# Converting a projection weight to bfloat16 one stage ahead, loading it on another queue, and issuing one input load ahead of a stage barrier

## The chip, the cores and the metric

The kernel runs on the 8 cores of one Trainium2 chip, as one program with no exchange between cores. Each core takes 1,024 query rows of one of two sequences; cores 0 to 3 hold sequence 0 and cores 4 to 7 sequence 1. The metric is the device time of the slowest core in microseconds (us), as the median of several runs.

## The reference, cut to what matters

```python
xn = _layernorm(x)                       # x: (2, 4096, 4096) float32
c_q = xn @ w_q_down                      # 4096 -> 1536
q_nope = c_q @ w_q_up_nope               # 32 heads x 128
q_rope = rope(c_q @ w_q_up_rope)         # 32 heads x 64
c_kv = xn @ w_kv_down                    # 4096 -> 512
k_rope = rope(xn @ w_k_rope)             # 4096 -> 64
q_lat = einsum('bhsd,hdr->bhsr', q_nope, wuk)
scores = q_lat . c_kv + q_rope . k_rope  # causal, / sqrt(192), softmax
out = (probs . c_kv) . wuv @ w_out
# FFN: router top-16 of 64, h = xn . A, out2 = (h * gates) . B
y = x + out + ffn(xn)
```

`w_kv_down` and `w_k_rope` lie side by side in one input called `wkvc`, 128 partitions x 32 x 576 values in float32 (9.44 MB; 4.72 MB as bfloat16). The tile for it in SBUF is `wkvcb`, in bfloat16.

## The kernel before, in words

Everything is emitted from Python into five in-order instruction lists (PE, DVE, ACT, POOL, SP) with semaphores. Transfers are issued by SP (`dma("sync", ...)`, queue q1, no conversion of type) and by POOL (`dma("gpsimd", ...)`, queue q0, which can convert float32 to bfloat16 on the way). Every transfer is spread over the core's 16 DMA engines. A helper on line 308 issues them all, so the profile has that one line for each; the tiles tell them apart.

The stages, in order of time in the profiled execution:

- 0 to 720 us: layer norm of the core's own rows, the projections to c_q, the router, the experts' first half, and `b_proj` for the 32 heads of q_nope (stage "qn"). For each head POOL loads a weight slice `wbuf<-wqn`; PE multiplies into one of two pairs of PSUM banks; `qn_evac` copies the pair to `qn_stg` on DVE (even heads) or ACT (odd heads), and SP stores that to DRAM (`qnope_scr<-qn_stg`). Each such copy waits on the semaphore `ysb` for *all* stores issued before it. `wqr_hook(oi)` is called after each slice load; at heads 3, 7, ..., 31 it makes POOL load one of eight parts of `wqrb`.
- 712 to 882 us: the rope half of q, for 8 blocks `tc` of 128 rows. SP loads two small tables (`ctab`, `stab`), PE multiplies into banks 0 to 3 (the banks that the last two q_nope heads used), DVE applies the rotation (lines 620 to 629), PE transposes (line 644), DVE and ACT in turn copy to `tr_stg`, and SP stores 128 KB (`qrope_scr<-tr_stg`). Here too each copy waits for all earlier stores (`ysb`).
- `stage_barrier()`: every engine waits until every semaphore has reached its count, those of all transfers too.
- 882 to 1547 us: stage A, over the 4,096 rows of the whole sequence, in 16 tiles of 256 rows. POOL loads `wkvcb` right behind the barrier. `emit_ln_stats_a` loads 128 rows of `xkv` (2 MB, as two halves) to `xbuf[slot]` on SP and takes the sums (DVE line 336, ACT lines 339 to 345); `emit_ln_stats_b` finishes the statistics and normalises (DVE line 385); `emit_ln_trans` transposes on PE (line 402) to `slabA`; `a_kv_tile` multiplies by `wkvcb` (lines 717, 721). Both chunks of a tile have their sums taken (`emit_ln_stats_a` twice) before the statistics of the first are finished.
- 1547 to 4660 us: a barrier, then attention over 32 heads; in its first 16 heads POOL converts `wout` and `b2` in DRAM to bfloat16 (`cast`, one after another on the semaphore `gc`).
- 4660 to 5286 us: a barrier, then the output projection and the experts' second half.

Of the kernel before, what the change touches and what calls it, by code (L numbers as in the profile page):

```python
# [10 lines left out]
BF16 = mybir.dt.bfloat16  # L11
# [83 lines left out]
def view3(t_ap, inner):  # L95
    n = t_ap.shape[1] // inner
    return t_ap.rearrange("p (c j) -> p c j", c=n)


def build_nc():  # L100
    nc = bass.Bass("TRN2", target_bir_lowering=False)

    def din(name, shape, dtype=F32):
        return nc.dram_tensor(name, list(shape), dtype, kind="ExternalInput").ap()

    XKV = din("xkv", (S_, D_))
# [4 lines left out]
    WKVC = din("wkvc", (128, 32, 576))  # L111
# [18 lines left out]
    KTS = nc.dram_tensor("ckvtm_scr", [128, S_ // 128, KVL_], BF16, kind="Internal").ap()  # L130
    ATS = nc.dram_tensor("attn_scr", [128, H_, NTOK], BF16, kind="Internal").ap()
    WOUTC = nc.dram_tensor("wout_c", [16, 128, 8192], BF16, kind="Internal").ap()
    B2C = nc.dram_tensor("b2_c", [16, 128, 2048], BF16, kind="Internal").ap()
    OUT = nc.dram_tensor("out_own", [NTOK, D_], F32, kind="ExternalOutput").ap()

    es = ExitStack()
    with es:
# [6 lines left out]
        kb = KB(sems)  # L144
# [31 lines left out]
        def pview(pool, name, shape, dtype, off):  # L176
            nbytes = int(np.prod(shape[1:])) * mybir.dt.size(dtype)
            assert off % 32 == 0, name
            assert off + nbytes <= pool.shape[1], (name, off, nbytes)
            base = nc.lookup_mloc(pool).addr  # L180
            return nc.alloc_sbuf_tensor_at(name, list(shape), dtype,
                                           offset=base + off)
# [12 lines left out]
        wkvcb = pview(pool1, "wkvcb", (128, 18432), BF16, 32768)  # L195
# [35 lines left out]
        xbuf = [pview(poolf, "xbuf0", (128, 4096), F32, 0),  # L231
                pview(poolf, "xbuf1", (128, 4096), F32, 16384)]
# [54 lines left out]
        def bank(i):  # L287
            return ps[i // 2][:, (i % 2) * 512:(i % 2) * 512 + 512]
# [7 lines left out]
        def t_run(fns):  # L296
            for f in fns[:-1]:
                kb.raw("tensor", f)
            return kb.t(fns[-1])
# [3 lines left out]
        def use(nm):  # L303
            uses[nm] = uses.get(nm, 0) + 1
            return uses[nm]

        def dma(eng, sem_name, out_ap, in_ap):
            kb.op(eng, lambda e, o=out_ap, i=in_ap: e.dma_start(out=o, in_=i),
                  inc=(sem_name, 16))
            return 16 * use(sem_name)  # L310
# [10 lines left out]
        lnfree = {("V", 0): 0, ("V", 1): 0, ("S", 0): 0, ("S", 1): 0}  # L321

        def R(nm, slot):
            return ST[nm + ("Z" if slot else "")]

        def emit_ln_stats_a(xsrc_row_ap, slot):
            sx = f"yx{slot}"
            kb.wait("sync", "V", lnfree[("V", slot)])
            kb.wait("sync", "S", lnfree[("S", slot)])
            dma("sync", sx, xbuf[slot][:, 0:2048], xsrc_row_ap[:, 0:2048])  # L330
            nl = dma("sync", sx, xbuf[slot][:, 2048:4096], xsrc_row_ap[:, 2048:4096])
            xb = xbuf[slot][:]
            kb.wait("vector", sx, nl)
            kb.drain("vector")
            kb.raw("vector", lambda e, xb=xb, slot=slot:
                   e.reduce_sum(R("xsum", slot), xb[:, 0:2048], AX))
            kb.wait("scalar", sx, nl)
            kb.drain("scalar")
            kb.raw("scalar", lambda e, xb=xb, slot=slot: e.activation(
                sqd[:], xb[:, 0:2048], ACT.Square, accum_out=R("xsqa", slot)))  # L340
            kb.drain("scalar")
            kb.raw("scalar", lambda e, xb=xb, slot=slot: e.activation(
                sqd[:], xb[:, 2048:4096], ACT.Square, accum_out=R("xsqb", slot)))
            kb.drain("scalar")
            s_sq = kb.s(lambda e, xb=xb, slot=slot: e.activation(
                sqd[:, 0:2048], xb[:, 2048:4096], ACT.Identity,
                accum_out=R("xsum2", slot)))
            lnfree[("S", slot)] = s_sq
            lnpend[slot] = (xb, s_sq)
# [67 lines left out]
        def stage_barrier():  # L417
            snap = dict(kb.cnt)
            for eng in KB.ENGS:
                for nm, v in snap.items():  # L420
                    kb.wait(eng, nm, v)

        xnfmB3 = view3(xnfmB[:], 1024)
        cq3 = view3(cqfm[:], 1024)
        for ch in range(8):
            emit_ln_stats_a(XOWN[ch * 128:(ch + 1) * 128, :], ch % 2)
            if ch > 0:
                vp = emit_ln_stats_b((ch - 1) % 2)
                emit_ln_trans((ch - 1) % 2, vp, xnfmB3, (ch - 1) * 128,
                              (4, 5, 6, 7))  # L430
# [49 lines left out]
        slot = 0  # L480
# [79 lines left out]
        b_proj(0, 8, xnfmB3, 32, None, cq_lhs, h_src, h_evac, "h")  # L560
        h_tm = kb.cnt["T"]

        def wqr_hook(oi):
            if oi % 4 == 3 and oi // 4 < 8:
                j = oi // 4
                if j == 0:
                    kb.wait("gpsimd", "T", h_tm)
                dma("gpsimd", "gq",
                    wqrb[:, j * 3072:(j + 1) * 3072],
                    WQR[j // 4][:, (j % 4) * 3072:(j % 4 + 1) * 3072])  # L570

        def qn_src(oi, slot):
            return (wbuf[slot][:, 0:1536], WQN[oi])
# [19 lines left out]
        for tc in range(8):  # L593
# [41 lines left out]
            for gi in range(4):  # L635
# [19 lines left out]
                dst = QRS[:, gi * 4:(gi + 1) * 4, tc * 128:(tc + 1) * 128]  # L655
                dma("sync", "ysb", dst, view3(tr_stg[sslot][:], 128))

        b_ysb = 16 * uses.get("ysb", 0)
        stage_barrier()

        slab3P = [view3(slabA2[0][:], 256), view3(slabA2[1][:], 256)]
        ckvfm3 = view3(ckvfm[:], 4096)
        wkv_loaded = dma("gpsimd", "g0", wkvcb[:], WKVC[:].rearrange("p c j -> p (c j)"))

        _gclast = [0]

        def cast(dst, srcw):
            if _gclast[0]:
                kb.wait("gpsimd", "gc", _gclast[0])
            _gclast[0] = dma("gpsimd", "gc", dst, srcw)  # L670

        lnfree[("V", 0)] = kb.cnt["V"]
        lnfree[("V", 1)] = kb.cnt["V"]
# [7 lines left out]
        def a_ln_stats_tile(t):  # L681
            for i4 in range(2):
                ch = t * 2 + i4
                emit_ln_stats_a(XKV[ch * 128:(ch + 1) * 128, :], ch % 2)
            return [emit_ln_stats_b((t * 2) % 2), emit_ln_stats_b((t * 2 + 1) % 2)]

        def a_ln_trans_tile(t, vxs):
# [7 lines left out]
        def a_kv_tile(t):  # L695
            slot = t % 2
            slab3 = slab3P[slot]
            tsl = t % 2
            kf = ktab_free[tsl]
            if kf:  # L700
                kb.wait("sync", kf[0], kf[1])
            dma("sync", f"yt{tsl}", view3(ktabc[tsl][:, 0:128], 64),
                COSK[t * 256:(t + 1) * 256, :].rearrange("(i p) j -> p i j", p=128))
            ktab_ns[t] = dma("sync", f"yt{tsl}", view3(ktabs[tsl][:, 0:128], 64),
                             SINK[t * 256:(t + 1) * 256, :].rearrange("(i p) j -> p i j", p=128))
            kb.wait("tensor", "g0", wkv_loaded)
            lv, ls = ln_done[t]
            kb.wait("tensor", "V", lv)
            kb.wait("tensor", "S", ls)
            kb.guard(0, 1, 2, 3, 4)  # L710
            fns = []
            for dc in range(32):
                for rc in range(4):
                    fns.append(lambda e, o=bank(rc)[:, 0:256],
                               l=view3(wkvcb[:], 576)[:, dc, rc * 128:(rc + 1) * 128],
                               r=slab3[:, dc, :], st=(dc == 0), sp=(dc == 31):
                               e.matmul(o, l, r, start=st, stop=sp))  # L717
                fns.append(lambda e, o=bank(4)[0:64, 0:256],
                           l=view3(wkvcb[:], 576)[:, dc, 512:576],
                           r=slab3[:, dc, :], st=(dc == 0), sp=(dc == 31):  # L720
                           e.matmul(o, l, r, start=st, stop=sp))  # L721
            tm = t_run(fns)
            kv_done[t] = tm
            return tm
# [103 lines left out]
        krdup_done = dma("sync", "ya", krdup[64:128, :], krdup[0:64, :])  # L828
        a_ysa = 16 * uses.get("ysa", 0)
        stage_barrier()  # L830

        ckvtm3 = view3(ckvtm[:], 512)
# [52 lines left out]
        def issue_loads(h):  # L885
# [8 lines left out]
            if h < 16:  # L894
                cast(WOUTC[h], WOUT[h])
                cast(B2C[h], B2[h])

# [373 lines left out]
        for dt in range(16):  # L1271
            ws = dt % 2
            gw = f"gw{ws}"
            kb.wait("gpsimd", "T", gw_free[ws])
            dma("gpsimd", gw, woutb[ws][:], WOUTC[dt])
            ngw = dma("gpsimd", gw, b2b[ws][:], B2C[dt])
            kb.wait("tensor", gw, ngw)
# [174 lines left out]
```

How the kernel before makes its waits and increments, by code:

```python
        def wrapped(e, fn=fn, h=h, amt=amt):  # L49
            fn(e).then_inc(h, amt)
# [3 lines left out]
    def wait(self, eng, nm, val):  # L54
        if val is None or val <= 0:
            return
        h = self.sems[nm]
        self.ops[eng].append(lambda e, h=h, v=val: e.wait_ge(h, v))
```

## Time and profile before

| what | us |
|---|---|
| median of 3 runs (5287.18 to 5734.02) | 5287.41 |
| the profiled execution | 5287.49 |
| its span on the slowest core (core 6) | 5286.0 |
| spans of the 8 cores | 5250.4 to 5286.0 |
| busy on the slowest core: PE / DVE / ACT | 4649.3 / 2305.2 / 1693.7 |

The span runs from the first to the last instruction of a core; the execution's own time is 1.5 us more. Busy shares are means over stages with different limits, so an edit is priced in its own stage, from what ends the waits there.

### The profile page before, as it was taken

What the parts mean: (1) busy time and instruction counts of PE and PEld (TensorE: products, weight loads), DVE (VectorE), ACT (ScalarE), POOL (GpSimd) and SP (SyncE); (2) the same over time, 40 slices, a digit from 0 to 9 for tenths busy, and PEclk for the clock granted to TensorE, in tenths of its full rate; (3) what the DMA queues carried; (4) which work ended last, traced back from release to release, by engine and by line L of the source; (5) the groups of instructions that cost most, each with busy time, mean ns of one, the idle gap of its engine ahead of it and who ended that gap; (6) DMA issues with size and microseconds to landing.
All of it is one profiled execution on the core that took longest, in us unless ns stands there. A gap on an engine that the chain in (4) does not pass through costs nothing.

```text
span 5286.0 us, 78953 instructions; the slowest of 8 cores (5250.4 to 5286.0 us)
## 1 busy us (share of the span) xinstructions
PE 4649.3 (88%) x27024; PEld 2202.6 (42%) x27024; DVE 2305.2 (44%) x4604; ACT 1693.7 (32%) x3075; POOL 100.5 (2%) x194
## 2 busy tenths in 40 slices
PE   1879874788858999999999999999999999969999
PEld 1434331444433444444444444444444444434444
DVE  3110032444424555555555555556555555511111
ACT  4100000454513444444444444444444444400000
POOL 0000000000000000000000000000000000000000
PEclk7889987899988999999999999999999999989999
DMA  4334734333336303303311000000000000054343
GB/s 129 64 54 89 128 69 88 105 137 112 133 116 89 49 5 53 53 6 48 53 24 30 13 13 1 13 13 1 13 13 13 1 13 5 1 166 129 124 136 104
DMA packets 151798, 318.09 MB, mean 60 GB/s; under 512 B 36736, under 2 KB 110720, under 8 KB 133440
## 3 DMA queue, kind: packets, MB, share of 16 engines
q0 software_dynamic: 24672, 137.38, 14.5%
q1 hardware_dynamic: 126752, 175.66, 10.2%
q8 instruction: 243, 3.98, 0.3%
q14 instruction: 131, 1.07, 0.1%
HBM read 363.59 MB, written 85.98 MB: 85 GB/s over the span
## 4 chain that ended last, share of the span: by engine, by line
PE 76%; DMA 9%; DVE 6%; issue 3%; ACT 3%; DVEq 2%; ACTq 0%; SPq 0%; POOL 0%; POOLq 0%
PE ps L1030 18%; PE ps L955 18%; PE ps L1294 8%; PE ps L717 6%; PE ps L458 6%; PE ps L961 5%; PE ps L1008 4%; DMA qnope_scr<-qn_stg 3%; PE ps L721 2%; PE ps L1302 2%; DVEq L61 2%; PE ps L964 2%; DMA xbuf<-xown 1%; DVE stats L973 1%; ACT probsb L994 1%
## 5 line engine op out<-in xcount | busy, mean ns | idle before, releaser
L955 PE MATMUL ps<-ckvfm,qlat 128*128 128x512 bf16 x4608 | 1111.0, 382 | 54.3 <-ACT probsb L994 29.7
L1030 PE MATMUL ps<-ckvtm,probsT 128*128 128x512 bf16 x4608 | 1102.1, 380 | 15.6 <-DVE stats L973 7.6
L994 ACT ACTIVATE probsb<-ps,stats 128x1024 bf16<-128x1024 f32 (+1 forms) x640 | 652.3, 1019 | 520.7 <-DVE stats L973 520.7
L1030 PEld LDWEIGHTS ps<-ckvtm,probsT 128*128 128x128 bf16 x4608 | 418.5, 98 | 599.1 <-issue 174.8
L955 PEld LDWEIGHTS ps<-ckvfm,qlat 128*128 128x128 bf16 x4608 | 421.3, 98 | 494.3 <-issue 104.7
L1294 PE MATMUL ps<-attn_cat,woutb 128*128 128x512 bf16 x2048 | 452.5, 382 | 40.1 <-DMA b2b<-b_c 26.8
L978 DVE TENSOR_REDUCE stats<-ps 128x1 f32<-128x1024 f32 (+1 forms) x384 | 419.1, 1092 | 35.6 <-issue 0.9
L1008 PEld LDWEIGHTS ps<-idb,probsb 128*128 128x128 bf16 x4608 | 309.7, 98 | 154.0 <-issue 6.8
L86 ACT COPY probsT<-ps 128x1024 bf16<-128x1024 bf16 x320 | 296.3, 926 | 227.6 <-PE ps L1008 227.5
L1008 PE MATMUL ps<-idb,probsb 128*128 128x128 bf16 x4608 | 361.9, 219 | 0.0
L961 PE MATMUL ps<-krdup,qropefm 64*128 64x512 bf16 x1152 | 358.7, 383 | 0.0
L717 PE MATMUL ps<-slabA,wkvcb 128*128 128x256 bf16 x2048 | 336.6, 290 | 9.2 <-DVE krf L758 7.5
L973 DVE TENSOR_REDUCE stats<-ps 128x1 f32<-128x1024 f32 (+1 forms) x256 | 296.5, 1158 | 102.1 <-PE ps L961 80.3
L1294 PEld LDWEIGHTS ps<-attn_cat,woutb 128*128 128x128 bf16 x2048 | 201.0, 98 | 279.1 <-issue 47.9
L402 PE MATMUL ps<-idb,xn_tm 128*128 128x128 bf16 x1280 | 105.6, 240 | 236.4 <-DVE xn_tm L385 201.0
L1317 DVE COPY dsb<-ps 128x512 f32<-128x512 f32 x64 | 41.3, 686 | 551.0 <-PE ps L1302 551.0
L458 PE MATMUL ps<-xnfmB,wbuf 128*128 128x512 bf16 x1280 | 278.6, 381 | 1.4 <-ACT xnfmB L86 1.4
L991 ACT ACTIVATE stats<-stats 128x1 f32<-128x1 f32 x384 | 77.9, 203 | 623.0 <-DVE stats L984 623.0
L1040 DVE SCALAR_TENSOR_TENSOR accb<-accb,stats,ps 128x512 f32<-128x512 f32 x192 | 143.5, 748 | 288.5 <-PE ps L1030 285.5
L85 DVE COPY probsT<-ps 128x1024 bf16<-128x1024 bf16 x320 | 201.6, 630 | 37.7 <-PE ps L1008 37.7
L458 PE MATMUL ps<-cqfm,wbuf 128*128 128x512 bf16 x768 | 177.5, 391 | 32.3 <-DMA wbuf<-wqn 26.0
L717 PEld LDWEIGHTS ps<-slabA,wkvcb 128*128 128x128 bf16 x2048 | 165.8, 101 | 94.5 <-issue 23.3
(144 smaller groups left out, 3856.1 us busy)
## 6 DMA issues: line engine op xcount, KB each, us to landing
xbuf<-xkv SPq DMA_DIRECT2D x64, 1024.0 KB, 10.3
wout_c<-wout POOLq DMA_DIRECT2D x16, 2048.0 KB, 21.1
woutb<-wout_c POOLq DMA_DIRECT2D x16, 2048.0 KB, 9.1
xbuf<-xown SPq DMA_DIRECT2D x16, 1024.0 KB, 7.0
xdb<-xown SPq DMA_DIRECT2D x64, 256.0 KB, 5.6
out_own<-outb SPq DMA_DIRECT2D x64, 256.0 KB, 2.4
wbuf<-wqd POOLq DMA_DIRECT2D x12, 1024.0 KB, 8.5
wbuf<-wqn POOLq DMA_DIRECT2D x32, 384.0 KB, 5.9
```

Of the source, the lines that this page charges most:

```text
L85: return e.tensor_copy(d, s)
L86: return e.copy(d, s)
L458: e.matmul(o, l, r, start=st, stop=sp))
L717: e.matmul(o, l, r, start=st, stop=sp))
L955: st=(rc == 0): e.matmul(o, l, r, start=st, stop=False))
L961: sp=(not diag): e.matmul(o, l, r, start=False, stop=sp))
L973: v_mx = kb.v(lambda e, b=nm4[i4x]: e.reduce_max(b, pp[:, 0:wid], AX, negate=True))
L978: kb.raw("vector", lambda e: e.reduce_max(ST["negmg"], pp[:, 0:wid], AX, negate=True))
L994: e.activation(o, i, ACT.Exp, bias=b, accum_out=l))
L1008: e.transpose(o, i, idb[:]))
L1030: e.matmul(o, l, r, start=st, stop=sp))
L1294: st=(fc == 0): e.matmul(o, l, r, start=st, stop=False))
```

## The change

Three edits. A DRAM tensor `WKVCC` takes a bfloat16 copy of `wkvc`, made by POOL with `cast` directly behind the last part of `wqrb`, in head 31 of the q_nope stage. Behind the barrier, SP (no longer POOL) loads `wkvcb` from `WKVCC` in two halves, before the loads of the second chunk of `xkv`. The first chunk of `xkv` is loaded by SP ahead of the barrier, behind the last store of the rope stage; for that, the barriers leave out the semaphores `yx0` and `yx1`.

```diff
+    WKVCC = nc.dram_tensor("wkvc_c", [128, 18432], BF16, kind="Internal").ap()
...
-        def emit_ln_stats_a(xsrc_row_ap, slot):
+        def emit_ln_stats_a(xsrc_row_ap, slot, preloaded=None):
             sx = f"yx{slot}"
-            kb.wait("sync", "V", lnfree[("V", slot)])
-            kb.wait("sync", "S", lnfree[("S", slot)])
-            dma("sync", sx, xbuf[slot][:, 0:2048], xsrc_row_ap[:, 0:2048])
-            nl = dma("sync", sx, xbuf[slot][:, 2048:4096], xsrc_row_ap[:, 2048:4096])
+            if preloaded is None:
+                ...
+            else:
+                nl = preloaded
...
             for eng in KB.ENGS:
                 for nm, v in snap.items():
+                    if nm in ("yx0", "yx1"):
+                        continue
                     kb.wait(eng, nm, v)
...
         def wqr_hook(oi):
...
                     wqrb[:, j * 3072:(j + 1) * 3072],
                     WQR[j // 4][:, (j % 4) * 3072:(j % 4 + 1) * 3072])
+                if j == 7:
+                    cast(WKVCC[:], WKVC[:].rearrange("p c j -> p (c j)"))
...
         b_ysb = 16 * uses.get("ysb", 0)
+
+        kb.wait("sync", "V", lnfree[("V", 0)])
+        kb.wait("sync", "S", lnfree[("S", 0)])
+        dma("sync", "yx0", xbuf[0][:, 0:2048], XKV[0:128, 0:2048])
+        a_pre_nl = dma("sync", "yx0", xbuf[0][:, 2048:4096], XKV[0:128, 2048:4096])
+
         stage_barrier()
...
-        wkv_loaded = dma("gpsimd", "g0", wkvcb[:], WKVC[:].rearrange("p c j -> p (c j)"))
+        kb.wait("sync", "gc", 16)
+        dma("sync", "ya", wkvcb[:, 0:9216], WKVCC[:, 0:9216])
+        wkv_loaded = dma("sync", "ya", wkvcb[:, 9216:18432], WKVCC[:, 9216:18432])
...
-                emit_ln_stats_a(XKV[ch * 128:(ch + 1) * 128, :], ch % 2)
+                emit_ln_stats_a(XKV[ch * 128:(ch + 1) * 128, :], ch % 2,
+                                preloaded=(a_pre_nl if ch == 0 else None))
...
-            kb.wait("tensor", "g0", wkv_loaded)
+            kb.wait("tensor", "ya", wkv_loaded)
```

The function `cast`, as before, waits on POOL for the previous cast and issues one converting transfer; it is only defined earlier in the file.

## Rows read from the trace of the kernel before

**Rows 1.** The page: busy share in 40 slices of 132 us, PE's clock.

```profile
PE   1879874788858999999999999999999999969999
...
PEclk7889987899988999999999999999999999989999
```

**Rows 2.** Busy time by stretch: engines (instructions), PE clock, DMA share, GB/s; stage A's start.

```profile
882.00:905.00 23.00, 0.00 (x0) 0.00 (x0) 0.00 (x0) 0.00 (x0) 0.72 (x1) 0.50 0.95 193
905.00:927.00 22.00, 0.00 (x0) 0.00 (x0) 2.38 (x2) 6.12 (x7) 0.00 (x0) 0.50 0.89 204
927.00:950.00 23.00, 7.69 (x65) 6.51 (x66) 13.81 (x22) 11.42 (x15) 0.00 (x0) 0.50 0.52 169
```

**Rows 3.** The chain that ended last, around the barrier: start us, us, what.

```profile
879.05 2.47 DMA qrope_scr<-tr_stg
...
881.94 0.34 SPq L308
...
883.27 43.49 DMA xbuf<-xkv
...
926.89 1.91 ACT sqd L339
...
949.93 1.01 PE ps L717 x4
```

**Rows 4.** A transfer issued in 882 to 884 us: engine, count, KB, us to landing.

```profile
wkvcb<-wkvc POOLq DMA_DIRECT2D x1, 4608.0 KB, 42.2
```

**Rows 5.** DMA queues in 966 to 979 us: GB/s in 40 slices; packets, MB, share.

```profile
GB/s 0 151 101 151 328 277 429 454 454 378 378 403 403 454 328 252 378 252 202 277 277 277 429 202 176 202 252 227 378 227 277 403 403 403 403 454 429 429 429 393
...
q1 hardware_dynamic: 572, 4.11, 95.4%
```

**Rows 6.** The same view, 1568 to 1582 us.

```profile
q1 hardware_dynamic: 129, 4.03, 97.2%
```

**Rows 7.** The chain that ended last, end of q_nope and start of rope.

```profile
712.59 2.13 DMA qnope_scr<-qn_stg
714.80 1.02 ACT qn_stg L86
...
716.73 2.19 DMA stab<-sinq
719.07 0.69 DVE tba L620
```

**Rows 8.** Timeline, same stretch: start, us, engine, line, operation [idle before <-what ended it].

```profile
701.89 0.54 POOL L308 DMA_DIRECT2D wqrb<-wqr  x1
...
714.80 1.01 ACT L86 CAST qn_stg<-ps 128x1024 bf16<-128x1024 f32 x1 [10.90 <-DMA qnope_scr<-qn_stg]
```

**Rows 9.** Transfers issued in 701 to 703 us, as in Rows 4.

```profile
wqrb<-wqr POOLq DMA_DIRECT2D x1, 768.0 KB, 9.0
```

**Rows 10.** A store issued in 703 to 704 us, beside that load.

```profile
qnope_scr<-qn_stg SPq DMA_DIRECT2D x1, 256.0 KB, 7.2
```

**Rows 11.** Two converting copies within DRAM, issued at 1662 and 1991 us.

```profile
wout_c<-wout POOLq DMA_DIRECT2D x1, 2048.0 KB, 19.9
...
wout_c<-wout POOLq DMA_DIRECT2D x1, 2048.0 KB, 23.1
```

**Rows 12.** DMA queues while such a copy runs, 1808 to 1822.5 us: packets, MB, share.

```profile
q0 software_dynamic: 48, 1.57, 83.7%
q1 hardware_dynamic: 48, 0.10, 2.0%
```

**Rows 13.** Transfers issued in 1802.5 to 1803.5 us, with such a copy among them.

```profile
wout_c<-wout POOLq DMA_DIRECT2D x1, 2048.0 KB, 22.5
attn_scr<-attnstg SPq DMA_DIRECT2D x1, 256.0 KB, 22.3
```

**Rows 14.** DMA queues while wkvcb loads, 890 to 920 us.

```profile
q0 software_dynamic: 224, 4.13, 81.9%
q1 hardware_dynamic: 222, 1.69, 18.0%
```

More of the change, by code:

```diff
@@ L324, in R @@
             return ST[nm + ("Z" if slot else "")]
-        def emit_ln_stats_a(xsrc_row_ap, slot):
+        def emit_ln_stats_a(xsrc_row_ap, slot, preloaded=None):
             sx = f"yx{slot}"
-            kb.wait("sync", "V", lnfree[("V", slot)])
-            kb.wait("sync", "S", lnfree[("S", slot)])
-            dma("sync", sx, xbuf[slot][:, 0:2048], xsrc_row_ap[:, 0:2048])
-            nl = dma("sync", sx, xbuf[slot][:, 2048:4096], xsrc_row_ap[:, 2048:4096])
+            if preloaded is None:
+                kb.wait("sync", "V", lnfree[("V", slot)])
+                kb.wait("sync", "S", lnfree[("S", slot)])
+                dma("sync", sx, xbuf[slot][:, 0:2048], xsrc_row_ap[:, 0:2048])
+                nl = dma("sync", sx, xbuf[slot][:, 2048:4096],
+                         xsrc_row_ap[:, 2048:4096])
+            else:
+                nl = preloaded
             xb = xbuf[slot][:]
@@ L561, in build_nc, with cast @@
         h_tm = kb.cnt["T"]
+        _gclast = [0]
+        def cast(dst, srcw):
+            if _gclast[0]:
+                kb.wait("gpsimd", "gc", _gclast[0])
+            _gclast[0] = dma("gpsimd", "gc", dst, srcw)
         def wqr_hook(oi):
@@ L662, in build_nc @@
         ckvfm3 = view3(ckvfm[:], 4096)
-        wkv_loaded = dma("gpsimd", "g0", wkvcb[:], WKVC[:].rearrange("p c j -> p (c j)"))
[L665 to L670, printed above, removed]
+        kb.wait("sync", "gc", 16)
+        dma("sync", "ya", wkvcb[:, 0:9216], WKVCC[:, 0:9216])
+        wkv_loaded = dma("sync", "ya", wkvcb[:, 9216:18432], WKVCC[:, 9216:18432])
         lnfree[("V", 0)] = kb.cnt["V"]
```

## The prediction

> **What bounds the kernel now.** I read the page's slices first. PE is busy nine tenths or more nearly everywhere from the fourteenth slice on, and thin in the sixth and seventh (660 to 925 us, 7 and 4 tenths), with a lower clock there too [rows 1]. The change touches only that thin region, so the 88% of PE says nothing about its worth; what counts is what ends the waits at two places.
>
> The first place is the start of stage A. By stretch, PE does nothing from 882 to 927 us, at the lower clock level (0.50), while the DMA engines are busy 95% and 89% [rows 2]. The chain of waits names one transfer there: SP issues at 881.94, right behind the landing of the last rope store issued at 879.05 (2.47 us), then 43.49 us of `xbuf<-xkv` until ACT starts on the second chunk at 926.89. From there to the first `wkvcb` matmul at 949.93 it is 23.0 us of statistics, transposes and copies [rows 3]. The weight load issued by POOL at the same time takes 42.2 us to land [rows 4]; it is not awaited itself, but it holds the DMA engines while the chunks wait for them.
>
> The second place is the seam between q_nope and rope, 712 to 728 us. In the chain stand the store of head 30 (712.59, 2.13 us), the copy of head 31 on ACT (714.80), then `stab` (2.19 us), then the first rotation on DVE at 719.07 [rows 7]. The timeline says the same: the ACT copy stood 10.90 us idle until a store landed, not until PE was done [rows 8]. So this stretch runs at the latency of small transfers on q1, and only because they land in some 2 us.
>
> **Part one: the load leaves q0, the first chunk starts earlier.** Removed: 9.44 MB read and 4.72 MB written on q0. Added behind the barrier: 4.72 MB on q1, between chunk 0 (2.10 MB) and chunk 1 (2.10 MB); 8.9 MB in one queue, with nothing beside it. In order of time:
>
> - Chunk 0 is issued behind the last rope store, at about 879.5 rather than 881.94: 2.4 us earlier. Its waits on V and S were met hundreds of us before, and the barrier still waits for the store (the two transfers in front of it on SP cost about 0.4 us each, less than the 2.47 us it waits anyway).
> - The first byte moves about 2 us after the issue, by the latency of a lone small transfer (2.13 us in [rows 7]): 881.5.
> - The rate of q1 by itself: 4.11 MB in 13 us (316 GB/s) for `xkv` [rows 5] and 4.03 MB in 14 us (288 GB/s) for the loads of the next stage [rows 6]. I take 316, since the nearer row has the same kind of transfer: 8.9 / 0.316 = 28.2 us, so chunk 1 lands at about 910 instead of 926.9.
> - Behind the landing, the 23.0 us to the first matmul [rows 3] stay: the second chunk's sums still come first on DVE and ACT. The weights are in before chunk 1, being ahead of it in the queue. SP's two new issues stand before chunk 1's loads and the tables of tile 0; the tables are needed tens of us later, so this costs only what the sum holds. The wait for `gc` on SP is met long before.
>
> Gain: 926.9 - 910 = 17 us. Bounds: at the best slices of [rows 5] (about 430 GB/s) the 8.9 MB take 21 us and the gain is 24; at the 288 of [rows 6] they take 31 and it is 14; I go down to 12, since the slices of [rows 5] have a stretch near 200 to 280. Leaving `yx0` and `yx1` out of the later barriers is worth nothing: the last `xkv` loads have been used by then, and what those barriers wait for is the compute behind them. Once PE works on tile 0, all that follows in stage A hangs on that time and moves as one.
>
> **Part two: the conversion in DRAM.** It is new work of 9.44 MB read and 4.72 MB written, issued by POOL 0.5 us behind the last `wqrb` part (701.89 [rows 8]). That part lands 9.0 us later, at 710.9 [rows 9], and the conversion is behind it in the same queue. Nothing behind it on POOL is late: the next thing there is the barrier.
>
> How long: a `wout` part of 2048 KB takes 19.9 to 23.1 us to land [rows 11]. Taking off 2.1 us of fixed latency [rows 7] and scaling by 4608/2048 = 2.25 gives (19.9 - 2.1) x 2.25 = 40 us, at the long end 47. It would hold the engines from 710.9 to about 751.
>
> Who has to get past it: this is where the change costs. While a `wout` conversion runs, q0 and q1 move 48 packets each in 14.5 us; those of q0 are of 33 KB, those of q1 of 2 KB [rows 12]. So each of the 16 engines takes one packet of either queue in turn, and a small one of q1 gets by once in 14.5/3 = 4.8 us. A 256 KB store has 128 such packets, 8 an engine, and needs 8 turns, 39 us, or the end of the conversion if that is sooner. The trace has this very case: a 256 KB store issued with the conversion landed after 22.3 us, the conversion after 22.5 [rows 13]. In the q_nope stage it is seen in small: a store beside a 768 KB `wqrb` load takes 7.2 us [rows 10] against 2.13 alone.
>
> The Trainium skill ("DMA: Bandwidth & Descriptors", section "Queues, rings and completion order") says that a DMA engine round-robins between the queues with work at packet granularity; the trace agrees, with 48 packets against 48. A byte-fair sharing would let the 0.26 MB store by in a few us, and the sum would be that of the first rival below.
>
> Laid on the seam: head 30's store is issued at 712.59, the conversion has 9 packets per engine (288 KB at 33 KB), and the store gets its 8 packets in between them, landing at about 746 instead of 714.7. Only then does ACT copy head 31; then come its store, `ctab` and `stab`, all in q1 behind it, let through as the conversion ends at 751. DVE's first rotation, 4.3 us behind the copy before (714.80 to 719.07), starts at 751.5 instead of 719.07: 32 us late. Were the conversion cut into smaller packets, the store would land earlier and `stab` would be what waits: the first rotation needs 24 packets of q1 per engine behind each other, so the end of the conversion stays the bound. PE has the matmuls of banks 0 and 1 done; those of banks 2 and 3 wait for head 31's copy and take 24 x 0.22 = 5 us, about 10 at the lower clock level, beside 2.2 us of DVE for each bank: at most 2 to 4 us more, which I leave in the range. From there the rope stage goes as before, 32 us later, and nothing in it has slack to give back: the chain there is of small stores, DVE and tables [rows 7].
>
> Bounds of the 32: the conversion may be faster. `wkvcb`'s own conversion moved 4.13 MB in 30 us with 81.9% of the engines' time [rows 14], so 4.72 MB alone would take about 4.72/4.13 x 30 x 0.82 = 28 us; end at 739, 20 us late. At 47 us of duration it is 39 late. I stay near 40 us of duration, because [rows 11] are the rows with DRAM on both sides.
>
> **Sum**, against the profiled execution's 5287.5 (the median of the runs shown is 5287.4): +32 - 17 = +15, so 5302. The first part is right where it was meant to be, and the second gives more than that back, 170 us earlier.
>
> **Rivals.**
>
> - *The conversion is hidden* (small stores pass beside it; only its 0.2 to 2 us of crowding remain). For it: the rope stage moves only small stores and tables that land in some 2 us [rows 7], so there is bandwidth in plenty. Against: [rows 12, 13]. It gives -17: 5270, faster than before. The point from which it decides: the seam's delay must be under 17 us, that is, the conversion must end before 736, or a store take under 10 us beside it.
> - *A stall as forecast, and no gain at stage A*: bfloat16 rows on q1 move no faster than the mix before did, chunk 1 lands at 927 again, the cost stays: 5287.5 + 32 = 5319. For it: chunk 1 is now behind 4.72 MB in one queue, where before only packets in turn stood between. Against: the rates of [rows 5] and [rows 6].
> - *A short conversion*: at the rate of [rows 14], +20 - 17 = +3: 5291, no change to speak of.
>
> **Chances and range.** Forecast with its bounds of both terms (20 - 24 = -4 up to 39 - 12 = +27, so 5283 to 5315): 0.80, the short conversion being 0.15 of it. Hidden: 0.12. No gain: 0.08. The range 5281 to 5317 leaves out the last two. About 2% (106 us) is what a measurement can tell from no change here; no case reaches it: within 2% 0.98, faster 0.01, slower 0.01. The sign is the real question: slower by some us 0.8.
>
> **What would show it.** In the profile after: `wkvc_c<-wkvc` from POOL at 702.4, some 40 to 50 us to landing; the store of head 30 at 30 us or more to landing in place of 2.1; an idle of over 30 us of ACT ahead of its last `qn_stg` copy; the first `tba` at about 751; the rope stage's last store at about 911; then the transfer entry of the chain at stage A some 27 to 29 us long in place of 43.5, and the first `wkvcb` matmul at about 965 in place of 949.93 (15 us later), with the rest shifted by the same. Wrong if the store at 712.6 lands within 10 us, if the conversion's packets are so quick that the first `tba` is before 736, or if chunk 1 takes over 40 us.

## The result, and the profile after

| | us |
|---|---|
| before, median of 10 runs | 5287.95 |
| changed kernel, median of 10 runs | 5317.11 |
| ratio, with its 95% interval | 1.0049 (1.0038 to 1.0061) |
| profiled execution after, and its span (core 3) | 5312.3, 5310.7 |

The changed kernel is slower, by 0.49% or some 26 us (20 to 32). A run now and then falls into a state of the chip in which a whole die is slower, which puts single executions some hundreds of us higher; the two medians of ten above hold such runs, and all ratios and all times below leave them out.

Another core ends last in each profile (core 6 before, core 3 after), and cores differ among themselves in when they reach a stage: the first rotations of the 8 cores lie within 18 us before and within 30 us after. So I compare core 3 with core 3, and, for sizes, the mean of the 8 cores.

The chain of waits of the changed kernel, core 3, from the last heads of q_nope to the first rotation (start us, us, what):

```profile
696.74 18.32 DMA qnope_scr<-qn_stg
715.14 1.24 DVE qn_stg L85
716.44 32.35 DMA qnope_scr<-qn_stg
748.87 1.02 ACT qn_stg L86
...
750.79 1.96 DMA stab<-sinq
752.89 0.69 DVE tba L636
```

The same view of the kernel before, on the same core:

```profile
698.59 7.43 DMA qnope_scr<-qn_stg
706.12 1.24 DVE qn_stg L85
707.41 4.10 DMA qnope_scr<-qn_stg
...
713.52 1.96 DMA stab<-sinq
```

The store of head 30, which [rows 7] show at 2.13 us on core 6, takes 32.35 us (4.10 on this core before); the store of head 29 ahead of it 18.32 (7.43 before). Nothing else on the chain grew: the copy on ACT is 1.02 us, the table 1.96. The transfers that stand against it, POOL's large ones issued in 696 to 697 us (engine, count, KB, us to landing), are these; [rows 9, 10] answer to them:

```profile
wkvc_c<-wkvc POOLq DMA_DIRECT2D x1, 4608.0 KB, 51.7
wqrb<-wqr POOLq DMA_DIRECT2D x1, 768.0 KB, 14.1
```

And this is what the two queues moved between 724 and 744 us (packets, MB, share of the engines' time), to be read beside [rows 12]:

```profile
q0 software_dynamic: 68, 2.23, 90.3%
q1 hardware_dynamic: 68, 0.14, 2.0%
```

68 packets each, 33 KB against 2 KB: one for one. In front of that stretch it is not so. The same view from just behind the store's issue, 716.5 to 724 us:

```profile
q0 software_dynamic: 26, 0.85, 106.4%
q1 hardware_dynamic: 1, 0.00, 0.1%
```

So for over 7 us the store moved next to nothing, and only then did its packets take turns. The store is done when the conversion is (716.44 + 32.35 = 748.8; the conversion was issued at 696.87, and 696.87 + 51.7 = 748.6).

The other place, the start of stage A, again the chain of core 3 after; [rows 3] answer to it:

```profile
916.56 25.77 DMA xbuf<-xkv
942.45 1.91 ACT sqd L344
...
965.08 0.64 PE ps L735 x4
```

The transfer entry is 25.77 us long in place of 43.49 on core 6 and of 40.99 on core 3 before. The start of the matmuls with `wkvcb`, after and then before, core 3 (duration ns min/median/max, first and last start):

```profile
L735 PE MATMUL ps<-slabA,wkvcb x2048: 269/273/421, 965.1 to 1553.6; 128*128 128x256 bf16 x187
```

```profile
L717 PE MATMUL ps<-slabA,wkvcb x2048: 269/273/421, 944.6 to 1531.7; 128*128 128x256 bf16 x187
```

Their durations are unchanged and the stretch from first to last is 587 to 589 us in both: stage A moved as one. The following table is worked out from such rows, one for each of the 8 cores, as their mean: first and last start of `tba` (the rotations), first start of a `wkvcb` matmul, and the distance of the last two, which holds only the end of the rope stage, the barrier and the start of stage A. The last column is the distance from POOL's issue of the last `wqrb` part to the first `tba`, which holds only the seam.

| kernel | first `tba` | last `tba` | first `wkvcb` matmul | last `tba` to it | last `wqrb` issue to first `tba` |
|---|---|---|---|---|---|
| before | 715.0 | 864.2 | 942.8 | 78.6 | 18.5 |
| changed | 750.8 | 900.2 | 962.0 | 61.8 | 55.8 |
| e1: conversion alone | 748.0 | 896.6 | 975.0 | 78.4 | 55.5 |
| e2: conversion early | 710.8 | 861.6 | 924.2 | 62.6 | 17.2 |
| e3: preload alone | 711.9 | 861.2 | 937.4 | 76.2 | 18.0 |
| e4: early, chunk 1 first | 709.0 | 857.9 | 907.4 | 49.5 | 17.9 |
| e5: 1152-byte packets | 734.6 | 888.6 | 952.7 | 64.1 | 42.2 |
| e6: order alone | 710.4 | 859.9 | 924.2 | 64.3 | 18.3 |
| e7: parts in q_nope | 730.1 | 879.4 | 941.8 | 62.4 | 18.2 |
| e8: 4608-byte packets | 745.7 | 894.4 | 955.1 | 60.7 | 51.1 |

The seam costs 35.8 us by the first `tba`, or 37.3 by the last column, and the start of stage A gives back 16.8. From the first `wkvcb` matmul to the first of the last stage's woutb matmuls it is 3725.4 us before and 3727.2 after: nothing is gained or lost there.

The column of first `tba` has a spread by itself: before, e2, e3, e4 and e6 have no conversion near the seam and stand at 715.0, 710.8, 711.9, 709.0 and 710.4. A single profile of one kernel is good to some 4 us there. The two distances repeat far better: the last one is 17.2 to 18.5 us in the six kernels with no conversion behind the last `wqrb` part, and the one before it is 61.8, 62.6 and 62.4 in the changed kernel, e2 and e7, which start stage A alike.

### The profile page after: what moved, and what is told of

Read it like the earlier page. It is cut to its first block, busy times and chain, and to the rows that moved or that the text cites. A ratio compares the mean times of both kernels' runs of the same rounds, so it can differ in the third digit from the quotient of the medians.

```text
span 5310.7 us, 78937 instructions; the slowest of 8 cores (5266.4 to 5310.7 us)
## 1 busy us (share of the span) xinstructions
PE 4651.6 (88%) x27024; PEld 2202.5 (41%) x27024; DVE 2304.5 (43%) x4604; ACT 1693.6 (32%) x3075; POOL 100.2 (2%) x194
## 3 DMA queue, kind: packets, MB, share of 16 engines
q0 software_dynamic: 24560, 137.38, 14.1%
## 4 chain that ended last, share of the span: by engine, by line
PE 77%; DMA 8%; DVE 5%; issue 4%; ACT 3%; DVEq 2%; ACTq 0%; SPq 0%; POOL 0%; POOLq 0%
PE ps L1048 18%; PE ps L973 18%; PE ps L1312 8%; PE ps L465 6%; PE ps L735 6%; PE ps L979 5%; PE ps L1026 4%; PE ps L739 2%; DMA qnope_scr<-qn_stg 2%; PE ps L1320 2%; DVEq L61 2%; PE ps L982 2%; DMA xbuf<-xown 1%; DVE stats L991 1%; DVE qlat L91 1%
```

## The experiments

**e1: the conversion alone.** Everything else as before.

```diff
+                if j == 7:
+                    cast(WKVCC[:], WKVC[:].rearrange("p c j -> p (c j)"))
```

> The kernel before with one thing added: the conversion of wkvc in DRAM behind the last wqrb part, in head 31 of the q_nope stage. Nothing reads the copy; wkvcb is loaded by POOL behind the barrier as before. Stall theory (one packet of each queue in turn, so the small stores wait for the end of the conversion): the first rotation 32 to 38 us late as in the changed kernel, the whole kernel 5288 + 36 = 5324 us. Rival (the changed kernel's delay comes from elsewhere, the conversion is hidden): 5288 to 5290 us. Rival of byte-fair sharing: the stores land within 5 us each, some 10 us in all, 5298.

Measured: 5323.7 us (the kernel before beside it: 5281.9), ratio 1.0078 (1.0062 to 1.0094), so some 41 us slower (33 to 50). The first rotation is 33.0 us later than before by the table (748.0), 37.0 by the distance across the seam (55.5 against 18.5), where the changed kernel has 37.3; and the distance to the first `wkvcb` matmul is untouched (78.4 against 78.6). The chain on its core 6:

```profile
699.92 30.80 DMA qnope_scr<-qn_stg
730.81 1.24 DVE qn_stg L85
732.11 17.36 DMA qnope_scr<-qn_stg
749.55 1.02 ACT qn_stg L86
```

The whole cost stands without the other edits; both rivals fall. On this core it is head 29's store that meets the conversion first, and the two stores share the stall (30.80 + 17.36). The sum is set by the conversion, not by which store is caught.

**e2: the same conversion, in eight parts, in the c_q projection.** The rest as in the changed kernel (`...` marks what is left out here).

```diff
+        def wkv_hook(oi):
+            if 2 <= oi < 10:
+                j = oi - 2
+                dma("gpsimd", "gc", WKVCC[16 * j:16 * (j + 1), :],
+                    WKVC[16 * j:16 * (j + 1)].rearrange("p c j -> p (c j)"))
...
+        b_proj(0, 12, xnfmB3, 32, None, cq_lhs, cq_src, cq_evac, "cq",
+               after_load=wkv_hook)
...
-                if j == 7:
-                    cast(WKVCC[:], WKVC[:].rearrange("p c j -> p (c j)"))
```

> The changed kernel, but with the conversion in eight parts of 16 partitions (576 KB each), each issued by POOL behind a weight load of the c_q projection (groups 2 to 9 of 12), where no small store is awaited and a weight load of 1 MB takes 8.5 us out of some 19 per group. If the seam at 712 us is the whole cost: the seam is back at the time of before, the gain at the start of stage A stays (17 us), 5288 - 17 = 5271. If the gain at stage A is less than thought and the change costs little: nearer 5280. If each part delays the next weight load: 8 parts x up to 5 us, 5310.

Measured: ratio 0.9977 (0.9965 to 0.9988), 12 us faster than before (6 to 19). The seam is back, at 710.8, with the eight parts in front of it, so they cost nothing that shows where they are; the distance to the first `wkvcb` matmul keeps 16.0 us of the gain (62.6 against 78.6). The interval holds the 17 us that I forecast; its middle is 5 short.

**e3: the preload alone.** The kernel before, with the first chunk issued ahead of the barrier.

```diff
+        kb.wait("sync", "V", lnfree[("V", 0)])
+        kb.wait("sync", "S", lnfree[("S", 0)])
+        dma("sync", "yx0", xbuf[0][:, 0:2048], XKV[0:128, 0:2048])
+        a_pre_nl = dma("sync", "yx0", xbuf[0][:, 2048:4096], XKV[0:128, 2048:4096])
+
         stage_barrier()
```

> The kernel before with only the third edit: the first chunk of xkv is issued ahead of the barrier, and the barriers leave yx0 and yx1 out. My price for it was 2.4 us by itself: the engines start 2.4 us earlier and are busy from then until chunk 1 is in, 5288 - 2.4 = 5285.5. Rival: chunk 0 ahead of the barrier gets the engines alone for longer, but chunk 1 still shares with the converting load and lands as before: 5288.

Measured: ratio 0.9993 (0.9982 to 1.0004). The time can't tell 2.4 us from nothing. The distance to the first `wkvcb` matmul is 76.2 against 78.6, just 2.4 less, in one profile of each; kernels alike there differ by up to 0.8.

**e4: e2, with chunk 1 of `xkv` ahead of `wkvcb`.**

```diff
-        kb.wait("sync", "gc", _gclast[0])
-        dma("sync", "ya", wkvcb[:, 0:9216], WKVCC[:, 0:9216])
-        wkv_loaded = dma("sync", "ya", wkvcb[:, 9216:18432], WKVCC[:, 9216:18432])
...
                 pend_vx[t] = a_ln_stats_tile(t)
+            if t == 0:
+                kb.wait("sync", "gc", _gclast[0])
+                dma("sync", "ya", wkvcb[:, 0:9216], WKVCC[:, 0:9216])
+                wkv_loaded = dma("sync", "ya", wkvcb[:, 9216:18432],
+                                 WKVCC[:, 9216:18432])
```

> As the previous variant with the early conversion in eight parts, and in addition SP issues chunk 1 of xkv ahead of the two halves of wkvcb. If the start of stage A is set by chunk 1 and 23 us of work behind it, chunk 1 lands 4.72 MB / 0.316 = 15 us earlier, wkvcb lands where chunk 1 landed, and the first wkvcb matmul waits 23 us behind chunk 1: 15 us earlier again, 5271 - 15 = 5256. If wkvcb were the later of the two: at most 8 us of that, 5263. If something behind tile 0 sets the pace: 5271.

Measured: 5251.6 us (the kernel before beside it: 5281.9), ratio 0.9937 (0.9919 to 0.9955), 33 us faster than before (24 to 43) and some 59 faster than the changed kernel (0.9937 against 1.0049). This is the version that beats both. The distance to the first `wkvcb` matmul is 49.5: 13.1 us less than e2. In its chain (core 6) the transfer entry has become short, and the rest behind it is unchanged:

```profile
884.15 14.36 DMA xbuf<-xkv
898.64 1.91 ACT sqd L344
```

```profile
L738 PE MATMUL ps<-slabA,wkvcb x2048: 269/273/421, 921.3 to 1510.0; 128*128 128x256 bf16 x187
```

From ACT's start on chunk 1 to the first matmul it is 22.7 us, against 23.0 in [rows 3]: what PE waits for is still chunk 1 and the work behind it. The weights, now behind chunk 1, have landed by 912.6 us (issued at 885.6, 27.0 to landing at the most), 9 us before that matmul.

**e6: the order alone, with no copy and no preload.** The kernel before; POOL issues its own converting load when chunk 1 has landed.

```diff
-        wkv_loaded = dma("gpsimd", "g0", wkvcb[:], WKVC[:].rearrange("p c j -> p (c j)"))
...
             if t < 16:
                 pend_vx[t] = a_ln_stats_tile(t)
+            if t == 0:
+                kb.wait("gpsimd", "yx1", 16 * uses["yx1"])
+                wkv_loaded = dma("gpsimd", "g0", wkvcb[:],
+                                 WKVC[:].rearrange("p c j -> p (c j)"))
```

> The kernel before with the order alone changed: POOL issues its converting load of wkvcb when chunk 1 of xkv has landed, instead of at the barrier. No copy in DRAM, no preload. If stage A's start is set by chunk 1 with the engines shared: the two chunks land 4.2 MB / 0.316 = 13 us after they start, at about 897 instead of 926.9; wkvcb, alone, needs 28 to 31 us from there, about 927; the first wkvcb matmul then waits for the later of 897 + 23 = 920 and 927, so 927 instead of 949.9: 5288 - 23 = 5265. If the order did not matter: 5288; if the converting load alone takes the 42 us it took beside xkv: 939 and 5277.

Measured: ratio 0.9975 (0.9964 to 0.9987), 13 us faster than before (7 to 19); the distance to the first `wkvcb` matmul is 64.3, 14.3 less. That is less than the 23 I expected. The chain on core 6 says why:

```profile
884.54 12.61 DMA xbuf<-xkv
...
897.70 35.87 DMA wkvcb<-wkvc
...
934.47 0.58 PE ps L716 x2
```

The chunks came in 12.61 us, as forecast; the load then took 35.87 and not 28 to 31, and PE waited for that. The load did not have the engines to itself, as I had assumed: SP had begun to load the next tile's chunks. The queues from 897.5 to 933.6 us:

```profile
q0 software_dynamic: 272, 4.72, 80.8%
q1 hardware_dynamic: 218, 1.65, 14.7%
```

80.8% of 35.9 us is 29 us, the time forecast for the load by itself; that the rest of the delay is these chunks is read from this view and was not tested. Even so, this one moved instruction gives at stage A nearly what the change gives there with a copy, a second queue and a preload (16.8).

**e7: the eight parts, in the q_nope stage.** As e2, but at heads 1, 5, ..., 29.

```diff
         def wqr_hook(oi):
+            if oi % 4 == 1:
+                j = oi // 4
+                dma("gpsimd", "gc", WKVCC[16 * j:16 * (j + 1), :],
+                    WKVC[16 * j:16 * (j + 1)].rearrange("p c j -> p (c j)"))
+                _gclast[0] = 16 * uses["gc"]
```

> The changed kernel with the conversion in the same eight parts as in the early variant, but spread over the q_nope stage (heads 1, 5, ..., 29), where a small store is awaited for each head. If awaited small stores are what makes a place dear, each part costs up to its own 5 us: 8 parts up to 40 us, I expect 20 to 30, so 5288 - 17 + 25 = 5296. If being cut in parts is what saved the early variant, it costs nothing here either: 5271 to 5280.

Measured: ratio 1.0009 (0.9996 to 1.0022), so +5 us (-2 to +12). Against e2, which differs in the place alone, that is 17 us (1.0009 against 0.9977), and the first rotation says 19.3 (730.1 against 710.8). The seam itself is as before (18.2 us), so the delay lies ahead of it, among the heads. Being cut in parts is not what makes e2 free; the place is. The size is just under the 20 to 30 us that I expected: about 2 us for each part.

**e5: small packets.** The changed kernel with the copy's rows padded, so that each of the 4096 rows of 576 values is a packet of 1152 bytes.

```diff
-    WKVCC = nc.dram_tensor("wkvc_c", [128, 18432], BF16, kind="Internal").ap()
+    WKVCC = nc.dram_tensor("wkvc_c", [128, 32, 640], BF16, kind="Internal").ap()
...
-                    cast(WKVCC[:], WKVC[:].rearrange("p c j -> p (c j)"))
+                    cast(WKVCC[:, :, 0:576], WKVC[:])
```

The two loads of `wkvcb` read the padded rows.

> The changed kernel, with the bfloat16 copy laid out in DRAM with 640 instead of 576 values per row, so that the conversion goes row by row: 4096 packets of 1152 bytes (256 an engine) instead of 144 of 32 KB (9 an engine), same bytes, same queue, same place. Turn theory (an engine serves one packet of each queue in turn, so what counts is the time of one packet of the other queue): a turn costs some 0.16 us instead of 4.7, head 30's store lands within 5 us instead of 32, the first rotation is late by 5 to 8 us instead of 36, and the later small stores of the stage (32 packets an engine) by about 5 us each while the conversion lasts, some 17 us in all over the rope stage; the kernel about 5288 + 17 - 17 = 5288, up to 5300 if the conversion gets slower with small packets. Rival (the engines or DRAM are simply busy, the size of packets does not matter): the first rotation 36 us late, 5315.

Measured: ratio 1.0026 (1.0014 to 1.0039), +14 us, where the change has +26. The first rotation is 19.6 us late (23.7 by the distance across the seam, 42.2 against 18.5), neither 5 to 8 nor 36. The chain on its core 3, and the queues from 711 to 719 us:

```profile
710.02 10.54 DMA qnope_scr<-qn_stg
...
723.42 12.98 DMA stab<-sinq
736.54 0.69 DVE tba L636
```

```profile
q0 software_dynamic: 712, 0.82, 98.4%
q1 hardware_dynamic: 123, 0.23, 8.6%
```

Same bytes, same place, same queue, and the stall across the seam falls from 37.3 to 23.7 us: so the size of the packets counts, and "the engines are simply busy" does not explain it all. But the price per turn was wrong: q0 moved 712 packets for q1's 123, not one for one, and the store took 10.54 us.

**e8: packets in between, 4608 bytes.** The same edit with a copy of 128 x 8 rows of 2304 values, padded to 2368.

> The changed kernel with the conversion in packets of 4608 bytes (1024 of them, 64 an engine), between the 32 KB and the 1152 bytes tried so far. With 32 KB the two queues moved 68 packets each; with 1152 bytes 712 against 123, 5.8 to 1. If a turn of q0 is one packet at this size: 64 packets in some 40 us are 0.63 us each, head 30's store waits 8 turns and lands in 6 to 8 us, head 31's and the tables 24 turns, the first rotation 20 to 25 us late. If a turn of q0 is a fixed amount of some 6.7 KB (5.8 x 1152 bytes): one or two packets a turn, 5 to 10 us for the store, much the same. If q0 always gets 5.8 packets to one when they are not of 32 KB: 8 x 5.8 x 0.63 = 29 us for the store, first rotation 36 us late, 5315. The kernel as a whole, in the first two cases, 5300.

Measured: 5308.3 and 5315.1 us, beside 5283.6 and 5289.9 for the kernel before; two of each are too few for an interval. The first rotation is 30.7 us late (32.6 by the distance across the seam). The chain on its core 1:

```profile
704.52 15.13 DMA qnope_scr<-qn_stg
...
720.81 12.91 DMA qnope_scr<-qn_stg
...
735.11 13.90 DMA qnope_scr<-qn_stg
...
751.12 7.36 DMA stab<-sinq
```

The second of these stores, by the queues' packets: first 721 to 726 us, then 727 to 731.

```profile
q0 software_dynamic: 115, 0.53, 97.3%
```

```profile
q0 software_dynamic: 95, 0.44, 90.0%
q1 hardware_dynamic: 94, 0.19, 14.1%
```

Here the turns are one for one again (95 to 94), yet a store takes 13 to 15 us and not 6 to 8. The missing part is in front: for over 5 us after its issue at 720.81, q1 moves nothing at all. So a store issued into a running conversion is late to *start* too, and then each packet waits for its turn. I had only the second. The other traces show the same late start: next to nothing for over 7 us in the changed kernel (1 packet beside 26, above), and none beside 262 packets of q0 from 710 to 713 us in e5. Why small packets are served 5.8 to 1, and what happens in those first us, stays open; no run here tells it apart.

## Why the prediction was right, and where its sizes were off

The changed kernel was forecast at 5302 in a range of 5281 to 5317, slower by 15; it came out slower by 26 (20 to 32). Its median of ten is 5317.1, 0.1 above the end of the range; 5287.5 times the ratio is 5313.4, inside it. The direction and the mechanism hold; the seam was priced too low. By the steps of the prediction:

- *"The seam is where this change costs"*: shown by e1, which has that cost and nothing else, and by e2, where it is gone with the conversion moved. The rival "hidden" (-17, 5270) falls with e1.
- *The term of 32 us* is the one that was mis-sized. It measured 35.8, or 39 against the mean of the five kernels that have no conversion there (711.4), or 37.3 by the distance across the seam. Core 6, the core of [rows 7 to 10], shows which step failed. The `wqrb` part took 9.2 us there (9.0 in the sum), and the conversion, issued at 701.7, landed 48.9 us later, at 750.6 (751 in the sum): those two were right. But the prediction let head 30's store land at 746, and what is behind it get through as the conversion ends, with the first rotation at 751.5. The chain of core 6 has them one behind the other:

```profile
701.95 23.12 DMA qnope_scr<-qn_stg
...
726.46 24.56 DMA qnope_scr<-qn_stg
751.09 1.02 ACT qn_stg L86
...
753.02 3.64 DMA stab<-sinq
756.81 0.69 DVE tba L636
```

  The store of head 29 was caught first, so that of head 30 was issued at 726.46 and not at 712.59, and it was late to start as well (core 3: 1 packet in its first 7 us). It lands with the conversion, at 751.0, and the copy and the table come after it: the first rotation is at 756.8. Over the 8 cores it stands 5.0 us behind the conversion's landing, where the sum had 0.5.
- *The `wqrb` part in front* took 14.1 us on core 3, against 8.9 before. Not every core has this. If the times of all cores are taken from one zero, then in the four kernels with the whole conversion there (changed, e1, e5, e8) it is one core of each of the pairs 0 and 1, 2 and 3, 4 and 5, 6 and 7. In all 16 pairs the one that issues this part second, with its neighbour's conversion already issued, waits 13.7 to 15.5 us, and the first 8.6 to 10.8. In the kernels without a conversion there it is 8.6 to 11.3 on every core. That points to the neighbour's conversion as what the part meets; what the two cores share, no run here tells.
- *One store of head 30 is caught*: head 29's is, too (18.32 us, and in e1 30.80). It does not change when head 30's store lands, which the end of the conversion sets, but it is why nothing behind that store got through before.
- *The term of 17 us* measured 16.8 by the distance to the first `wkvcb` matmul, 16.0 in e2. Its 2.4 us for the preload measured 2.4 (e3, one profile). The load of `wkvcb` before chunk 1 is the bottleneck of what was left: e4 takes another 13.1 us by swapping them, where I had 15.
- *"The rest moves as one"*: first `wkvcb` matmul to the last stage's start, 3725.4 against 3727.2 us.
- *The sum* of the two terms by the means of the 8 cores is 35.8 - 16.8 = 19.0; at the last woutb matmul the means stand 21.6 apart (5260.0 and 5281.6), and the slowest cores' spans 24.7 (5286.0 and 5310.7). Of the 11 us by which the forecast fell short, 4 to 7 are the seam; the rest lies in which core is last and is within the spread of the runs (5303 to 5320 for the changed kernel), so I can't break it down further.
- *The rival "a stall and no gain at stage A"* (5319) has nearly the measured time, and is wrong: the distance to the first `wkvcb` matmul shows the gain in full. The total alone would have picked the wrong story.
- *The short conversion* (28 us, from [rows 14]) falls: from the landing of the `wqrb` part to that of the conversion it is 38 us on core 3 (710.5 to 748.6) and 40 on core 6 (710.4 to 750.6), for which I had taken 40. For a load into SBUF the 28 was not far off, since in e6 it took 80.8% of 35.9 us, 29 us; it was the wrong row for a copy within DRAM.
- *Turns of one packet*: exact for packets of 33 KB (68 and 68) and for 4608 bytes (95 and 94) once both move, not for 1152 bytes (712 and 123), and not behind the issue of a store in any of the three. The Trainium skill ("DMA: Bandwidth & Descriptors", section "Queues, rings and completion order") says that an engine goes round the queues packet by packet; with packets of 33 KB and of 4608 bytes these traces agree, once both move.

## What to carry to other kernels

Before a large transfer is moved to an "idle" stage, look at what small transfers that stage waits for, not at how busy its DMA engines are: here the seam, where PE and DVE wait for a few small stores and tables, was the dearest of the three places tried (+36 us), a PE-bound stage without awaited stores took the same bytes for nothing, and one with a store per head took 17 to 19. The last two had the copy in eight parts and the seam had it whole; how dear the parts would be at the seam was not tried. At a stage's start, order the loads by who needs them first and how long the work behind them is: the input chunk with 23 us of work behind it goes ahead of the weight, and in e6 that alone gave 14 us of the distance with no new work at all. When two edits of opposite sign meet in one change, compare distances within stages; the total fitted a wrong rival better than the right one.

## What the runs showed of the hardware that I had not expected

- A 256 KB store issued while a converting copy runs with 4608-byte packets moves nothing for over 5 us (115 packets of the other queue pass), then goes one for one, and lands after 12.9 to 15.1 us where it takes 2.1 alone. With 33 KB packets it is over 7 us (1 packet beside 26).
- Cutting the converting copy from 144 packets of 33 KB to 4096 of 1152 bytes hardly slows it (53.1 against 51.7 us to landing on core 3) and lets the other queue through sooner (10.54 against 32.35 us for the store), though at 5.8 packets to one.
- A 768 KB weight load that takes 8.6 to 11.3 us to land takes 13.7 to 15.5 on the second core of each pair (0 and 1, 2 and 3, 4 and 5, 6 and 7), in 16 pairs of 16, when the first has issued a 4.7 MB converting copy.
- The converting load into SBUF takes 35.9 us beside 1.65 MB of `xkv` (e6), only 6 less than beside 4.2 MB (42.2, [rows 4]), while the two chunks take 12.6 us without it and 43.5 beside it: `xkv` at its side cost it little, and it cost `xkv` a great deal.
